# Attention on one Trainium2 core: softmax sums divided in the packed, transposed layout after a round trip through DRAM

## The reference

```python
def _L0_attn_ref(hidden_states, Wq, bq, Wk, bk, Wv, bv, Wo, bo):
    ...
    q = split_heads(hidden_states @ Wq.T + bq)
    k = split_heads(hidden_states @ Wk.T + bk)
    v = split_heads(hidden_states @ Wv.T + bv)
    ...
    scores = jnp.einsum('bhqd,bhkd->bhqk', q, k) / math.sqrt(dh)
    causal = jnp.tril(jnp.ones((T, T), dtype=bool))
    scores = jnp.where(causal[None, None], scores, -jnp.inf)
    weights = jax.nn.softmax(scores, axis=-1)
    out = jnp.einsum('bhqk,bhkd->bhqd', weights, v)
    out = out.transpose(0, 2, 1, 3).reshape(B, T, H * dh)
    return out @ Wo.T + bo
...
x = x + _layernorm(_L0_attn_ref(_layernorm(x, axis=-1), L0_attn_Wq, ...), axis=-1)
x = x + _layernorm(_L0_ffn_ref(_layernorm(x, axis=-1), L0_ffn_gate_w, ...), axis=-1)
```

## Time and profile before

| | us |
|---|---|
| median of 3 runs | 2745.22 (2744.34 to 2745.78) |
| profiled execution, its own time | 2745.2 |
| its span, first to last instruction | 2743.5 |
| PE busy | 2519.6 (92%) |
| DVE busy | 2122.0 (77%) |
| ACT busy | 1419.8 (52%) |
| POOL busy | 983.8 (36%) |
| DMA queue of SP, share of 16 engines | 27.8% |

### The profile page before, as it was taken

How to read it: one execution, slowest core, us unless ns; L and a number is a source line. 1 busy time by engine, 2 the same in 40 slices (tenths; PEclk the granted TensorE clock), 3 DMA queues, 4 the chain that set the end, 5 groups by cost and what they waited for, 6 DMA issues and landing times. The chain is left out here.

```text
span 2743.5 us, 55677 instructions
## 1 busy us (share of the span) xinstructions
PE 2519.6 (92%) x19584; PEld 1213.8 (44%) x19584; DVE 2122.0 (77%) x6399; ACT 1419.8 (52%) x1838; POOL 983.8 (36%) x1083
## 2 busy tenths in 40 slices
PE   3899999999999999999999996099999999999997
PEld 1444544444454454454454443044444444444443
DVE  5999999999999999999999994735555455555454
ACT  3576776776766666767676664322222222222221
POOL 4454655655565565555556553000000000000000
PEclk8999999999999999999999999599999999999999
DMA  5332433433333433433442330401121111121111
GB/s 170 98 95 76 125 92 99 122 104 94 115 105 92 117 104 92 121 102 95 123 118 77 106 96 32 191 16 46 46 76 46 46 61 46 46 76 46 46 46 46
DMA packets 125314, 236.66 MB, mean 86 GB/s; under 512 B 11441, under 2 KB 94897, under 8 KB 111921
## 3 DMA queue, kind: packets, MB, share of 16 engines
q1 hardware_dynamic: 123056, 232.84, 27.8%
q10 hardware_dynamic: 2048, 1.05, 0.1%
HBM read 148.39 MB, written 84.41 MB: 85 GB/s over the span
## 5 line engine op out<-in xcount | busy, mean ns | idle before, releaser
L655 DVE CUSTOM_DVE_ANT_0 mx<-mx,causal 128x512 f32<-128x512 f32 (+3 forms) x2048 | 944.3, 518 | 47.4 <-PE mx L785 43.4
L491 ACT ACTIVATE probs<-ts,exp_scale 128x1024 f32<-128x1024 f32 x640 | 708.8, 1107 | 325.7 <-PE ts L799 323.7
L1229 DVE SCALAR_TENSOR_TENSOR hidden<-gu,up_scale,silu 128x512 f32<-128x512 f32 x176 | 131.9, 750 | 417.7 <-PE gu L1279 407.9
L1088 ACT ACTIVATE silu<-gu,gate_scale 128x512 f32<-128x512 f32 x176 | 120.9, 687 | 631.4 <-PE gu L1279 631.4
L1063 POOL TENSOR_TENSOR f_rstd<-f_var,f_neg_half 128x4 f32<-128x4 f32 x32 | 32.3, 1009 | 928.8 <-DVE f_var L1206 647.3
L403 POOL TENSOR_SCALAR_AFFINE_SELECT probs<-probs 128x512 f32<-128x512 f32 x512 | 311.7, 635 | 145.2 <-ACT probs L491 145.2
L1277 PE MATMUL gu<-f_xT_hi,gate_hi 128*128 128x512 f16 x704 | 268.0, 381 | 51.9 <-issue 51.9
L813 PE MATMUL xb<-probs,vs 128*32 128x512 f32 (+3 forms) x4096 | 305.5, 439 | 5.0 <-ACT shift_rows L497 3.0
L382 POOL TENSOR_TENSOR turned<-biased,sin_sb 64x512 f32<-64x512 f32 x128 | 170.0, 1328 | 327.3 <-ACT biased L476 320.9
L655 DVE DVE_READ_ACCUMULATOR2_ANT row_max<- 128x1 f32 x2048 | 285.5, 139 | 0.0
L1279 PE MATMUL gu<-f_xT_lo,gate_hi 128*128 128x512 f16 x704 | 267.8, 380 | 0.0
(11 more groups left out here) (148 smaller groups left out, 4469.3 us busy)
## 6 DMA issues: line engine op xcount, KB each, us to landing
slots<-half SPq DMA_DIRECT2D x260, 128.0 KB, 12.6
qT<-slots SPq DMA_DIRECT2D x128, 256.0 KB, 3.8
kT<-slots SPq DMA_DIRECT2D x128, 256.0 KB, 4.0
xn<-x SPq DMA_DIRECT2D x16, 1024.0 KB, 9.1
xr<-x SPq DMA_DIRECT2D x16, 1024.0 KB, 6.9
slots<-half SPq DMA_DIRECT2D x256, 64.0 KB
x<-xr SPq DMA_DIRECT2D x16, 1024.0 KB, 10.8
f_xn<-x SPq DMA_DIRECT2D x16, 1024.0 KB, 4.8
```

The source lines that it names most:

```text
L491: nc.scalar.activation(probs[:, g % 2, u, :, :], ts[:, :, :], ACT.Exp, scale=exp_scale[:, 0:1]).then_inc(ts_read, 1)
L655: last = nc.vector.tensor_tensor_reduce(out=scores, in0=scores, in1=causal[:, T - P * (qt + 1):T], scale=1.0, scalar=-3e38, op0=ALU.add, o ...
```

## The change

The weighed heads are no longer transposed back and divided token by token. ACT's copy `oT` (32 rows a head: 16 channels, the sum, padding) goes by one 256 KB transfer a group to a DRAM tensor `weighed`. When two groups are there, two transfers fetch them: `averaged` gets the 8 heads of 16 channels packed into 128 rows, and `sums` gets each head's sum row sixteen times over, so that both are 128x512 and stand row against row, channels by tokens, as the output projection wants them. DVE takes the reciprocal of `sums` (step 4 of groups 1, 3, 5, 7, table `FETCHED`), multiplies (step 0 of groups 0, 2, 4, 6, table `AVERAGED`), ACT makes the high part and adds the bias of the values there, DVE makes the low part. `turn_weighed`, `turn_attention` and `divide_by_sums` are gone.

Along with it: the two small steps that make the shifts go from DVE to POOL, as three operations, one group later in the order; the transfers that place the shifts go from ACT's queue to SP's; the values' copy out of PSUM goes from DVE to ACT, without its bias; the cosine reads the projection in PSUM with the bias instead of ACT's biased copy, stands before that step's maxima, and now is what frees the bank of the queries and keys; `BANK_USES` puts the transposed input in the bank of the shifts; the statistics of the input and the load of `xn` come one slot later; POOL's bodies 2 to 13 are written out instead of looped.

```diff
-            r = g % 2
-            BANK_USES += [(("qk",) + QUERIES_KEYS[g], r), (("s", (g + 1) % NG, (g + 1) // NG), 1 - r), (TURNED[g], r),
-                          (("av", (g - 1) % NG, (g - 1) // NG), 1 - r), (("o", (g - 1) % NG, (g - 1) // NG), 1 - r),
-                          (V_OR_OUT[g], r)]
+            BANK_USES += [(("qk",) + QUERIES_KEYS[g], r), (("s", (g + 1) % NG, (g + 1) // NG), 1 - r)]
+            if TURNED[g]:
+                BANK_USES.append((TURNED[g], 1 - r))
+                r = 1 - r
+            BANK_USES += [(("av", (g - 1) % NG, (g - 1) // NG), 1 - r), (V_OR_OUT[g], r)]
+            r = 1 - r
...
+        FREED_BY = {"qk": ((cosine_done, 8),), "v": ((v_read, NC),), "out": ((out_read, NT),),
+                    "s": ((shift_read, NG),), "av": ((oT_ready, NG),), "x": ((xT_ready, NC),)}
...
+        AVERAGED = {0: (2, -1), 2: (3, -1), 4: (0, 0), 6: (1, 0)}
+        FETCHED = {1: (3, -1), 3: (0, 0), 5: (1, 0), 7: (2, 0)}
...
+            def send_weighed(i, g):
+                ready, fetched = held(sp, NG * i + g + 1), held(sp, 32 * (NC * (i - 1) + g // 2 + 1))
+                sp.wait_ge(oT_ready, ready)
+                wait_if_any(sp, averaged_in, fetched)
+                sp.dma_start(weighed[g // 2, g % 2, :, :], oT[:, :]).then_inc(weighed_out, 16)
+
+            def fetch_weighed(i, c):
+                consumed = held(sp, NC * i + c)
+                sp.wait_ge(weighed_out, 16 * (NG * i + 2 * c + 2))
+                wait_if_any(sp, aT_ready, consumed)
+                heads = weighed[c, :, :, :].rearrange("g (h r) t -> (g h) r t", r=32)
+                sp.dma_start(sums[:, :], heads[:, DH:DH + 1, :].broadcast_to([8, DH, T])).then_inc(averaged_in, 16)
+                sp.dma_start(averaged[:, :], heads[:, 0:DH, :]).then_inc(averaged_in, 16)
...
+            def high_of_attention(i, c):
+                act.wait_ge(averaged_done, NC * i + c + 1)
...
+                nc.scalar.activation(aT_hi[:, (NC * i + c) % (NC + 2), :], averaged[:, :], ACT.Identity,
+                                     bias=bias_v[:, c:c + 1]).then_inc(aT_hi_done, 1)
...
+            def reciprocal_of_sums(i, c):
+                dve.wait_ge(averaged_in, 32 * (NC * i + c + 1))
+                nc.vector.reciprocal(sums[:, :], sums[:, :]).then_inc(recip_done, 1)
+
+            def average(i, c):
+                await_step(recip_done, NC * i + c + 1)
+                nc.vector.tensor_tensor(averaged[:, :], averaged[:, :], sums[:, :], ALU.mult).then_inc(averaged_done, 1)
...
             def cosine(i, n):
+                ct, which = divmod(n, 2)
                 wait_if_any(dve, qk_lo, 8 * i + n - 1)
                 dve.wait_ge(biased_ready, 8 * i + n + 1)
-                nc.vector.tensor_tensor(roped[:, n % 2, :], biased[:, n % 2, :], cos_sb[:, :],
-                                        ALU.mult).then_inc(cosine_done, 1)
+                nc.vector.scalar_tensor_tensor(roped[:, n % 2, :], xb[:, bank_of("qk", n), :], bias_qk[:, which, ct:ct + 1],
+                                               cos_sb[:, :], ALU.add, ALU.mult).then_inc(cosine_done, 1)
```

203 lines of the change are left out of this document (104 added, 99 removed).

## The result

| | before | after |
|---|---|---|
| median of the runs, us | 2745.16 (same chip) | 3002.55 (2997.12 to 3024.06, 4 runs) |
| ratio | | 1.0952, 95% interval 1.0898 to 1.1007 |
| profiled execution, its own time | 2745.2 | 3006.16 |
| its span | 2743.5 | 3004.4 |
| mean granted TensorE clock | 0.977 | 0.943 |

The change makes the kernel 257 us slower. The forecast was slower, by 65 us (2810, range 2660 to 2860): the direction was right, the size off by a factor of four, and the time lies outside the range.

The account below looks back on a forecast made before the run. PE and DVE, both full in the attention phase, were taken as the bound. Period 94.4 + 9.7 + 1.0 = 105.1 us, +4.0 in 15.5 periods: 2745.2 + 62 + 5 = 2812, stated as 2810 us, range 2660 to 2860.

Parts of the forecast that it names:

- Bound of the kernel before: Attention phase: PE busy 96.2 and DVE 95.3 of 100 us, both full, PE pacing the group.
- PE: what goes: PE's work falls 4.4 us a period and a 1.36 us wait goes: 101.1 to 95.3 us.
- bank terms: Step 2: 0.12 us saved in four groups without transposed input, 0.47 us lost in each of the other four.
- Price of the reciprocal: DVE's 128x512 reciprocal, in no row: taken as 3.1 us, from the 4- and 16-element operations.
- Both bounds: Limits on DVE's reciprocal of 512 elements: 0.7 us below, 7.9 us above.
- What PE then waits for: Even groups, late maxima and cosine: stalls 2.1, 0.8, 3.4, 3.4 us, plus 1.0 for collisions; period 105.1 us.
- the covered wait on ACT: PE's 0.88 us wait on ACT in group 4, covered if PE is late: period 94.4 instead of 95.3 us.
- Small terms: ACT and POOL: nothing; shifts in SP's queue: 0 to 1.5 us a period, hidden; end: +5 us once.
- PE's saving with its new waits, and the end: Period without stalls 95.3 us instead of 101.1; last sequence through DRAM and a long reciprocal, +5 us once.
- The reciprocal is cheap: Rival, chance 0.20: DVE's reciprocal takes 0.7 us, PE's saving stands, period 96.3 us, 2676 us in all.
- Late shifts as the bound: Rival fitting any case, no chance of its own: shifts late in SP's queue, up to +1.5 us a period, 23 us.
- Only the first stall counts: Rival, chance 0.10: cosine in time, PE loses only to late maxima; period 99.9 us, 2732 us in all.

Follow-up runs that it names:

- the fill: PE repeats score products in its stalls, same output: 2869.59 us on the changed kernel with early fetches, 2956.46 us on the changed kernel itself.
- the first experiments: Changed kernel with a 4-column reciprocal and no division, 2833.99 us; with shift transfers on ACT's queue, 3059.65 us; with both, 2853.69 us.

## Why the prediction was wrong, and what of it was right

**Bound of the kernel before.** Right: PE and DVE were both full, and a gain on one was worth what the other let through.

**PE: what goes.** The 0.73 us of step 3 went: steps 3 and 4 both last 1.94 to 1.99 us in the groups without a stall. The 1.36 us wait for the low part went too. In the best case of the change's own order (early fetch, short reciprocal, shifts on ACT) the period is all the same 99.2 us ((1392.96 - 103.87) / 13), where I had 95.3. The starts of the maxima, averaged by group over the periods between 400 and 1600 us, say where the rest is. Seven groups together take 83.4 us, before 88.0: 4.6 us saved, of 5.5 forecast for them. Their bank terms were a little short: step 2 with a transposed input grew by 0.51, 0.46 and 0.74 us in groups 0, 1 and 6, where I took 0.47, and without one it shrank by 0.04, where I took 0.12. Group 4 takes 15.7 us, before 13.1, where I had about 12.9. That is 2.8 of the missing 3.9 us a period, some 44 us in 15.5 periods, and it is the group behind the fetch that the load of `xr` delays.

**Price of the reciprocal.** Right within 8%: 3.35 us against 3.1. Both bounds held, and of the two values read from the 16-element row the larger was the nearer. The reading of the long cosine in the earlier trace rows is a rough one: it ends 0.54 us behind the POOL operation, a bit less than its own 0.68. Its consequence held: the cosine lost its long forms.

**What PE then waits for.** The stalls were forecast at 9.8 us a period net of the covered wait on ACT (105.1 against 95.3), 152 us; the measured cost of the length is 173. This agreement is partly luck: about 55 us of it are the clock, which I had not counted, so the stalls themselves were nearer 7.6 us a period. The places were right. With the fill, where the clock stays up, groups 0, 2 and 6 take 2.0, 1.0 and 3.1 us longer than with the short reciprocal, forecast 2.1, 0.8 and 3.4. Group 4 takes 0.2 us longer, forecast 3.4: there PE is late for transfers already. The episode above, with PE stopping for the maxima (1.32 us) and then for the cosine (2.51), has 3.8 us where 3.4 were forecast, but from a later start of DVE and of PE alike, so it shows the places and not the sum.

**The step that failed** is "Small terms". I checked the shifts' place in SP's queue and called their lateness hidden; the two fetches in the same queue I counted only as traffic ahead of them and never asked when they land themselves. They are issued only once the weighed heads are in DRAM, behind four other transfers, and DVE asks for them at the end of that very group. The text on DVE's block started the reciprocal 0.2 us into the even group without asking when its input lands. In the trace it started late (1.30 us in the episode, 103.8 us over the kernel), and everything that I had placed behind it came later: 78 us. With the shifts behind the same fetches (32 us) and the late group 4 (some 44), about 154 of the 190 us between the forecast 2812 and the measured 3002.55 stand behind transfers of that queue; the 44 is read from the trace of one run and not tried.

**The clock** was the other missing term. The prediction quoted a granted clock of 1.00 and kept it while it forecast four stalls a period. Their price is the wait plus the slow matmuls behind it, about 55 us for the reciprocal's.

**The sum, put right,** from measured differences:

| us | forecast | measured |
|---|---|---|
| PE's saving with its new waits, and the end | -85 (15.5 x 5.8, +5) | -26 (2719.48 against 2745.77) |
| shifts in SP's queue | 0 | +32 |
| length of the reciprocal | +152 | +173, about 55 of it by the clock |
| late fetches | no term | +78 |
| sum | +67 | +257 |

The four steps were taken in this order; in another order the shifts' part has the other sign, as the first experiments show, so it belongs to this path and not to the shifts alone.

**Rivals.** "The reciprocal is cheap" was priced at 2676 us. The change with a short one measured 2834 as it stands, 2752 with early fetches and 2719 with the shifts on ACT as well: this case too would have come out wrong, for the same missing term. "Late shifts as the bound" was priced at up to 23 us and is 32 in one order and below zero in another. "Only the first stall counts" was wrong: PE stops at both. My list of what would prove me wrong did hold "if PE waits for a transfer at the start of a group", which is what it does.

**Left open.** What group 4 would take with the load of `xr` out of the fetch's way was not tried by itself. That the added traffic also slows the transfers that were there before was not tried alone.

## What to carry to other kernels

A chain through DRAM has two prices, the transfers and the place of their issue in a queue. Before costing the consumer, write down when its input was issued, what is ahead of it in that queue, and when it lands; here that was 6.3 us for a fetch that the schedule gave 5.0. When PE is nearly full, as at 96% here, and a stall of a microsecond or two is forecast, ask what the matmuls behind it would take at half clock; the weighing took 4.50 us instead of 2.36. And the longest wait in a list may be the one that hides the real one: remove it and see whether the time follows. A wait that goes may also come back at a worse place: two kernels here waited as long as before and lost 57 and 20 us beside a lower clock.

An expensive elementwise operation belongs ahead of the spreading, not behind it: 32 columns instead of 512 made the reciprocal 0.34 us instead of 3.35, for one more small transfer each way.

## What the runs showed of the hardware

- DVE's reciprocal costs about 6.2 ns an element and partition beyond the smallest sizes: 178 ns at 4, 248 at 16, 344 at 32, 3353 at 512. (344 - 248)/16 = 6.0, (3353 - 344)/480 = 6.3. The one at 16 reads PSUM, the others SBUF.
- Added PE work in stalls made two kernels 46 and 55 us faster, by keeping the granted clock at 0.98 to 0.99 instead of 0.93 to 0.95 (400 to 1600 us).
- The second fetch of 256 KB, behind five other transfers of the same queue, was there 6.3 us after its issue began; with a 1 MB load and one fetch ahead of it, 8.6 us.
